# Which of two engines copies the transposed attention tiles out of PSUM, slot by slot

## The reference

```python
def attention(x, spatial, edge, Wq, Wk, Wv, Wo):          # 16 heads of 32
    q, k, v = split_heads(x @ Wq.T), split_heads(x @ Wk.T), split_heads(x @ Wv.T)
    a = einsum('bhnd,bhmd->bhnm', q, k) * D ** -0.5 + (spatial + edge)[:, None]
    row_nonzero = any(a != 0, axis=-1, keepdims=True)
    p = softmax(where(row_nonzero, a, -inf)); p = where(isnan(p), 0, p)
    return merge_heads(einsum('bhnm,bhmd->bhnd', p, v)) @ Wo.T

def experts(x, adj, ...):
    top1 = argmax(x.mean(axis=1) @ router_w + router_b, axis=-1)
    out = adj @ (x @ expert_w[top1])
    # batch norm over all graphs of one expert, then relu

x = layernorm(x + attention(x, adj, adj, Wq, Wk, Wv, Wo))
x = layernorm(x + experts(x, adj, ...))
```

## Time and profile before

| | us |
|---|---|
| median of 3 executions | 2518.1 (2517.59 to 2522.15) |
| profiled execution | 2520.1 |
| its span, first to last instruction | 2518.3 |
| mean granted TensorE clock | 0.951 of full speed |
| busy: PE, DVE, POOL, ACT | 2233.9, 1739.8, 1746.6, 1586.9 |
| copies `pt<-t_bank` on ACT (768) | 452.8 |
| copies `pt<-t_bank` on DVE (256) | 175.5 |

### The profile page before, as it was taken

How to read it: one execution, slowest core, us unless ns; L and a number is a source line. 1 busy time by engine, 2 the same in 40 slices (tenths; PEclk the granted TensorE clock), 3 DMA queues, 4 the chain that set the end, 5 groups by cost and what they waited for, 6 DMA issues and landing times.

```text
span 2518.3 us, 48708 instructions
## 1 busy us (share of the span) xinstructions
PE 2233.9 (89%) x14496; PEld 1721.1 (68%) x14496; DVE 1739.8 (69%) x4498; ACT 1586.9 (63%) x3762; POOL 1746.6 (69%) x3196
## 2 busy tenths in 40 slices
PE   3678899998989999998989999898989999898864
PEld 2456677776767777676767777676767777676653
DVE  2476776767686776768586776767677676867558
ACT  0456666666666666666666666666666666665447
POOL 0578777777777777677777777777777777777324
PEclk7789999999999999999999999999999999999987
DMA  6487465564747456464747556474846556473877
GB/s 219 129 270 252 120 201 175 171 198 139 221 126 251 129 175 194 158 194 130 241 127 228 151 180 187 142 217 130 250 119 205 173 168 198 135 224 102 313 283 286
DMA packets 213189, 472.66 MB, mean 188 GB/s; under 512 B 40832, under 2 KB 49024, under 8 KB 206144
## 3 DMA queue, kind: packets, MB, share of 16 engines
q1 hardware_dynamic: 212928, 469.55, 60.1%
HBM read 270.16 MB, written 65.01 MB: 133 GB/s over the span
## 4 chain that ended last, share of the span: by engine, by line
PE 74%; DVE 10%; issue 5%; ACT 3%; SPq 3%; POOL 3%; DMA 1%; DVEq 0%; POOLq 0%; ACTq 0%
PE t_bank L377 15%; PE p_bank L281 13%; PE p_bank L282 13%; PE p_bank L283 13%; PE o_bank L396 9%; PE s_bank L360 8%; SPq L773 2%; DVE att L541 2%; DVE xt L609 1%; POOL fold L742 1%; DVE x L609 1%; PE o_bank L387 1%; ACT att L453 1%; POOL fold L744 1%; ACT pt L515 1%
## 5 line engine op out<-in xcount | busy, mean ns | idle before, releaser
L742 POOL TENSOR_TENSOR fold<-att 128x256 f32<-128x256 f32 x1024 | 766.1, 748 | 492.9 <-DVE nmax L541 406.5
L541 DVE CUSTOM_DVE_ANT_0 att<-s_bank,adj_t 128x512 f32<-128x512 f32 x1024 | 695.7, 683 | 383.5 <-PE s_bank L360 382.5
L453 ACT ACTIVATE att<-att,nmax 128x512 f32<-128x512 f32 x1024 | 738.7, 722 | 181.8 <-POOL fold L742 166.3
L515 ACT ACTIVATE pt<-t_bank 128x512 f32<-128x512 f32 x768 | 452.8, 597 | 399.5 <-PE o_bank L396 268.9
L377 PE MATMUL t_bank<-ident,att 128*128 128x128 f32 x4096 | 637.6, 279 | 20.7 <-ACT pt L515 11.0
L377 PEld LDWEIGHTS t_bank<-ident,att 128*128 128x128 f32 x4096 | 507.1, 143 | 208.0 <-issue 77.6
L360 PE MATMUL s_bank<-k_stack,q_stack 128*128 128x512 f32 x1024 | 502.0, 491 | 73.0 <-DVE nmax L541 72.5
L744 POOL TENSOR_TENSOR fold<-fold 128x128 f32<-128x128 f32 x1024 | 500.5, 489 | 80.3
L749 POOL TENSOR_TENSOR fold<-fold 128x64 f32<-128x64 f32 x1024 | 356.3, 348 | 80.2
L360 PEld LDWEIGHTS s_bank<-k_stack,q_stack 128*128 128x128 f32 x1024 | 200.1, 195 | 92.2 <-DVE nmax L541 89.7
L396 PE MATMUL o_bank<-pt,v 128*32 128x256 f32 x4096 | 250.2, 385 | 5.4 <-issue 4.5
(11 more groups left out here) (359 smaller groups left out, 3659.2 us busy)
## 6 DMA issues: line engine op xcount, KB each, us to landing
q_stack<-qk_t SPq DMA_DIRECT2D x1024, 64.0 KB, 3.1
k_stack<-qk_t SPq DMA_DIRECT2D x1024, 64.0 KB, 2.0
qk_w<-qk_split SPq DMA_DIRECT2D x123, 512.0 KB, 4.8
slot_a<-expert_split SPq DMA_DIRECT2D x16, 2048.0 KB, 8.0
slot_b<-vo_split SPq DMA_DIRECT2D x15, 2048.0 KB, 8.2
slot_a<-vo_split SPq DMA_DIRECT2D x15, 2048.0 KB, 9.6
stage<-in_xT SPq DMA_DIRECT2D x16, 1024.0 KB, 5.6
adj_t<-in_adj SPq DMA_DIRECT2D x64, 256.0 KB, 7.5
```

Of the source, the lines that this page charges most:

```text
L453: eng.activation(att[:, u % 4, j, :], att[:, u % 4, j, :], ACT.Exp, bias=nmax[:, u % 4, j:j + 1], scale=-1.0, accum_out=rsum[:, u % 4, j:j ...
L515: eng.activation(pt[:, j, :, (u % 2) * P:(u % 2 + 1) * P], t_bank[r % 2][:, :].rearrange("p (m n) -> p m n", m=NT), ACT.Copy).then_inc(act ...
L541: eng.tensor_tensor_reduce(out=att[:, u % 4, j, :], in0=s_bank[r % 2][:, :], in1=adj_t[:, t, :], scale=-2.0, scalar=3.0e38, op0=ALU.add, o ...
L742: eng.tensor_tensor(fold1[:, :], a[:, 0:256], a[:, 256:512], ALU.add).then_inc(pool_fold1, 1)
```

## The change

In slots 5, 6, 7 and 8 ACT copies all four transposed tiles; in the other twelve slots DVE keeps the tile of j = 3. The one constant is replaced by a list of the steps that DVE copies, and the places that count copies (the waits of `pe_turn`, `pe_pv` and the last graph's O product) count by that list. Nothing else changes.

```diff
-DVE_TURNED = 3
+DVE_COPIES = [4 * u + 3 for u in range(16) if u not in (5, 6, 7, 8)]
...
-                wait(eng, act_pt, b, (HG - 1) * UNITS, 0)
-                wait(eng, dve_pt, b, UNITS, 0)
+                wait(eng, act_pt, b, STEPS - len(DVE_COPIES), 0)
+                wait(eng, dve_pt, b, len(DVE_COPIES), 0)
...
+        def dve_copied(r):
+
+            return sum(at < r for at in DVE_COPIES)
+
         def wait_turned(eng, b, r):
 
-            u, j = divmod(r, HG)
-            if j == DVE_TURNED:
-                wait(eng, dve_pt, b, UNITS, u + 1)
+            at = r % STEPS
+            back = (r - at) // STEPS
+            if at in DVE_COPIES:
+                wait(eng, dve_pt, b + back, len(DVE_COPIES), dve_copied(at) + 1)
             else:
-                wait(eng, act_pt, b, (HG - 1) * UNITS, (HG - 1) * u + j + 1 - (j > DVE_TURNED))
+                wait(eng, act_pt, b + back, STEPS - len(DVE_COPIES), at - dve_copied(at) + 1)
...
-            wait(eng, act_pt, b, (HG - 1) * UNITS, (HG - 1) * 2 * (pair + 1))
-            wait(eng, dve_pt, b, UNITS, 2 * (pair + 1))
+            wait(eng, act_pt, b, STEPS - len(DVE_COPIES), 2 * HG * (pair + 1) - dve_copied(2 * HG * (pair + 1)))
+            wait(eng, dve_pt, b, len(DVE_COPIES), dve_copied(2 * HG * (pair + 1)))
...
-                if attends and r >= 0 and j != DVE_TURNED:
+                if attends and r >= 0 and r not in DVE_COPIES:
...
-                if attends and r >= 0 and j == DVE_TURNED:
+                if attends and r >= 0 and r in DVE_COPIES:
```

## The result

The changed kernel takes 2507.0 us (2506.7 to 2507.4, 5 runs) against 2518.1 (2517.3 to 2522.2): a ratio of 0.9952, 95% interval 0.9938 to 0.9967. That is 11.1 us less. The forecast was 2504.0, 14.1 less, in a range of 2498 to 2514. In the two profiled executions the span went from 2518.3 to 2505.1, 13.2 less.

A forecast was written before the change was run, and what follows sets the result against it. PE was taken as the bound (74% of the chain), so only its waits for DVE or ACT count. 4.6 + 10.4 + 0.7 + 1.2 - 2.8 = 14.1 us off 2518.1 gave 2504.0, range 2498 to 2514.

The forecast's parts named there:

- Copy (5,3): Slot 5, step 3: the moved copy lies in idle time of DVE and ACT; gain 0, bound 0.6 us per graph lost.
- Copy (6,3): Slot 6, step 3: free on ACT, which starts slot 7 0.69 us earlier; PE's xt wait (3.54 us) is not shortened.
- Copy (7,3): Slot 7, step 3: value product at (8,0) stops waiting for it; mean 0.33 us over 14 graphs, 4.6 us gained.
- the clock: Slot 7, graphs 1 to 14: shorter graphs meet the 1.2 GHz stretch later; -2.8 us, bounds include +14 x (5.99 - 3.83)/2 = 15.
- the low stretch stands 0.4 us later in the mean: Step of the clock term: half-speed stretch after PE's standstill in slots 6 and 7 shifts later; 14 x 0.4 x 0.5 us lost.
- Copy (8,3): Slot 8, step 3: PE's waits for DVE in slot 9 shrink 0.69 us a graph, 10.4 us over graphs 1 to 15.
- Turn 0.24 earlier: Slot 9: PE's transposes of (9,1) come 0.24 us earlier; with scores of (9,2) 0.45 more, 0.69 us a graph.
- Graph 15: Last graph, slot 7: transposes of (7,1) wait for copy (6,3), and the logits follow one copy earlier; 0.7 us gained.
- Graph 0: First graph, slots 5 to 8: 0.69 us at slot 8 and some 0.5 at slot 5, 1.2 us gained (bounds 0 and 2.7).
- B: Rival: clock falls keep spacing and slot, so graphs can't stay shorter than 143.36 us; 2514 us, chance 0.15.
- D: Rival: slower, the low clock lasts 10 us and not 6.8 in graphs 1 to 14; 2528 us, chance 0.07.
- C: Rival: ACT's idle cover in slot 5 fails, 0.60 us lost behind copy (6,0) in 14 graphs; 2512.4 us, chance 0.06.

## Why the prediction was right, and its steps

**Copy (5,3), 0:** right, in the trace and alone on the chip. The cover held with 0.79 us of idle left.

**Copy (6,3), free but of no direct use:** right that PE's wait for xt stays (65.0 to 64.2 us). But alone it makes slots 7 and 8 together 1.8 us shorter in graphs 1 to 14.

**Copy (7,3), 4.6 us, and the clock, -2.8:** the place was right, the sizes were not, and the two can't be added as the prediction does. Together they were to give 1.8 us; slots 7 and 8 gave 6.3. The 4.6 rests on a mean wait of 0.33 us at (8,0), taken between 0.75 and 0. Over graphs 1 to 14 of before it is 0.22 us, 3.1 in all (0.04 in the changed kernel, where it is gone in ten graphs). Two steps of the clock term failed. One is "the low stretch stands 0.4 us later in the mean": it stands 0.6 us earlier. I had assumed that falls would go on past 5.8 us for a while. They come at 5.7 at the latest and then go back to 2.7, a place where none had been in graphs 1 to 14 of before. The other is "each microsecond more at half speed costs half a microsecond". In slot 7 it does, but up to a fall 5.0 us behind (7,0) slot 8 gives it back, because the product there waits for the copy. An earlier low stretch makes that wait longer, so the copy was worth more and the clock's place less than each was by itself: with slot 8's copy alone, the falls equally early, slots 7 and 8 gave 0.6 us, with all four 6.3. The bound of 15 us for the clock compared graph 1 with graph 14; against the mean of before (5.12 us of matmul time) it is 14 x (5.12 - 3.83) / 2 = 9. A part of slot 8's gain goes in graphs 3, 9 and 12, with an early fall: the first low part of x1 takes 0.99 us there and not 0.78.

**Copy (8,3), 0.69 us a graph, 10.4 us:** right place, wrong size. It gave 0.40 a graph, 5.6 us. Three steps of its working failed. "Turn 0.24 earlier" was read from the weight load, which runs ahead of the matmuls; the matmuls of (9,1) had started only 0.04 us late. The words "without the copy they start 0.69 us earlier" took the copy's length for the time that it held DVE, 0.60. And it left out the folds: the copy, which reads PSUM and took 0.67 to 0.69 us all 256 times, had kept two instructions with two SBUF operands further from POOL's first fold. The prediction had this rule in hand (the Trainium skill, "SBUF — State Buffer", section "Who interferes with whom") and priced it at up to 8 us, but left it out of the sum. The trace agrees with the rule: 0.46, 0.65 and 0.99 us for one instruction. The prediction named the low part of `ot` (+0.14 us) and missed the weights beside it (+0.34).

**Graph 15, 0.7:** the transposes of (7,1) came 1.6 us behind (7,0) and not 5.8, and the logits sooner, but PE then waits for ACT's copy of (7,0), and the value product meets a later low clock. Graph 15 in the changed kernel, the scores of (7,1) and the transposes of (7,2):

```profile
2285.54 0.51 PE L360 MATMUL s_bank<-k_stack,q_stack 128*128 128x512 f32 x1 [3.02 <-DVE nmax L546]
...
2288.46 1.08 PE L382 MATMUL t_bank<-ident,att 128*128 128x128 f32 x4 [2.42 <-ACT pt L520]
```

The scores come 5.2 us behind (7,0) and not 6.5, the transposes of (7,2) 8.1 and not 8.4. At (8,1) nothing is left (16.9 and 16.8). Slot 9 then gives 0.4 us in this graph too.

**Graph 0, 1.2:** can't be judged. It differs by -1.5 to +2.5 us between the traces of these kernels in ways that don't follow the copies.

So that the total is near is in good part luck: slot 9 gave 4 us too little in graphs 1 to 14, slots 7 and 8 4.5 too much. The places were right (the slots 7 to 9, and nothing in slot 5), the sizes were not. That the medians show 11.1 and the traces 13.2 has to do with the execution profiled of before, 2.0 above its median.

**The rivals.** B did not happen in the changed kernel, but it does with slot 7's copy alone, and with slot 6's in half of the graphs. D's longer low stretch (10.2 us) is seen there too; the graphs with it are 143.2 to 143.4 us long, like those just before it. C is out: 0.79 us of idle is left, and slot 5's copy alone costs nothing.

## What to carry to other kernels

When a stall is long enough to make the clock fall, the length of a loop and the spacing of the falls can lock together, and a gain in the stage behind the stall is paid back until the loop is shorter by more than the clock can take; so read where the low stretch lies in several iterations before pricing a gain behind it. Giving the stalled PE throw-away work took most of the question away here: the same change was worth 18 us with the clock held up, 11 without. Read neighbouring stages together: an earlier fall made slot 7 4.5 us shorter and slot 8 3.9 us longer, and only the copy moved out of slot 7 turned that into a gain. And an instruction that is taken away may have been the spacer between two engines that disturb each other; look what its followers will meet.

## What was not expected of the hardware

- The falls of the clock stood 143.36 us apart, and a loop near that length can lock to them. In the trace with slot 7's copy alone eight graphs in a row had their fall in the same place within 0.1 us (2.39 to 2.46 us behind (7,0)), with slot 6's alone five.
- The same DVE instruction with two SBUF operands (128x256) takes 0.46, 0.65 or 0.99 us, by the POOL fold beside it (almost empty, 128 or 256 columns), and does so the same way in each of 14 graphs.
- Four float32 products of 128x512 in the standstill behind (7,0) kept the granted clock at 1.00 through slot 7 in 8 or 9 of 14 graphs; in the others it was at 0.50 for 3.4 us and not 6.8.
